# Routed experts on one core: where tiles of x1 wait, which queue loads unit 7 of W2, and when a piece of W1 is loaded

## What is computed

```python
grouped = x.reshape(b, s // g, g, d)                        # groups of g = 32 tokens
logits = jnp.einsum('bntd,des->bntes', grouped, Wc) + bc + tie
perm = (logits == jnp.max(logits, axis=-3, keepdims=True))  # each expert takes one token of each group
permuted = jnp.einsum('bntd,bntes->bnesd', grouped, perm)
inner = jax.nn.relu(jnp.einsum('bnesd,esdf->bnesf', permuted, W1) + b1)
result_permuted = jnp.einsum('bnesf,esdf->bnesd', inner, W2) + b2
result = jnp.einsum('bnesd,bntes->bntd', result_permuted, perm)
x = x + jnp.tanh(g_ffn[0]) * result                         # the input of this layer is layernorm(x)
```

## Time and profile before

| | us |
|---|---|
| median of 3 runs | 1896.14 |
| lowest and highest | 1892.81, 1897.17 |
| profiled execution, time | 1897.31 |
| profiled execution, span | 1895.3 |
| TensorE busy in the span | 1670.7 (88%) |
| VectorE busy | 1321.8 (70%) |
| ScalarE, POOL busy | 708.7, 752.8 |
| TensorE's mean granted clock | 0.944 |

### The profile page before, as it was taken

How to read it: one execution, slowest core, us unless ns; L and a number is a source line. 1 busy time by engine, 2 the same in 40 slices (tenths; PEclk the granted TensorE clock), 3 DMA queues, 4 the chain that set the end, 5 groups by cost and what they waited for, 6 DMA issues and landing times.

```text
span 1895.3 us, 51938 instructions
## 1 busy us (share of the span) xinstructions
PE 1670.7 (88%) x22488; PEld 1157.6 (61%) x22488; DVE 1321.8 (70%) x1944; ACT 708.7 (37%) x907; POOL 752.8 (40%) x896
## 2 busy tenths in 40 slices
PE   7899999999999999997797778887887888877985
PEld 4677777777777777775565435653465446543652
DVE  6677777777777777775376657676676567665766
ACT  3523333223332333322444344344434444434442
POOL 3467777777777777773111111111111111111101
PEclk9999999999999999998998899888998889888997
DMA  7533444444434444435665677566866686567655
GB/s 269 167 110 134 165 145 166 144 165 149 171 132 151 142 160 144 153 120 178 189 227 182 211 252 248 194 201 231 263 194 199 227 273 204 194 219 263 233 159 190
DMA packets 184435, 356.27 MB, mean 188 GB/s; under 512 B 23824, under 2 KB 33808, under 8 KB 178704
## 3 DMA queue, kind: packets, MB, share of 16 engines
q1 hardware_dynamic: 179600, 319.39, 50.9%
q10 hardware_dynamic: 4608, 33.56, 4.9%
HBM read 274.17 MB, written 78.71 MB: 186 GB/s over the span
## 4 chain that ended last, share of the span: by engine, by line
PE 58%; DMA 16%; DVE 11%; SPq 8%; issue 4%; ACT 2%; POOL 0%; DVEq 0%; ACTq 0%
PE ps L1400 14%; PE ps L877 10%; PE ps L924 10%; PE ps L1374 8%; DMA xin<-x_scratch 6%; DMA gat<-in_W 5%; PE ps L937 5%; DMA out<-gat 4%; SPq L1194 4%; PE ps L892 3%; PE ps L950 2%; DVE mx L675 2%; SPq L1190 2%; PE ps L1423 2%; PE ps L911 1%
## 5 line engine op out<-in xcount | busy, mean ns | idle before, releaser
L189 POOL TENSOR_SCALAR xin<-xin,r_all,nb_all 128x512 f32<-128x512 f32 x128 | 98.8, 781 | 624.2 <-DMA xin<-x_scratch 624.0
L1307 DVE STREAM_TRANSPOSE res<-res 128x2048 f32<-128x2048 f32 x128 | 292.0, 2295 | 0.1
L1278 ACT ACTIVATE res<-ps 128x1024 f32<-128x1024 f32 x160 | 157.9, 1024 | 288.8 <-PE ps L1423 288.8
L1268 ACT ACTIVATE gat<-ps 128x1536 f32<-128x1536 f32 (+1 forms) x128 | 172.2, 1345 | 214.2 <-PE ps L1374 214.2
L877 PE MATMUL ps<-xTh,qh 128*128 128x512 f32 x512 | 209.2, 409 | 5.5 <-DVE qs L692 1.9
L877 PE MATMUL ps<-xTh,ql 128*128 128x512 f32 x512 | 200.3, 391 | 0.0
L877 PE MATMUL ps<-xTl,qh 128*128 128x512 f32 x512 | 200.1, 391 | 0.0
L1374 PE MATMUL ps<-sel,xin 32*128 32x128 f32 x4096 | 158.9, 291 | 36.7 <-ACT gat L1268 22.5
L1418 PE MATMUL ps<-b2s,rowk 32*128 32x512 f32 x512 | 75.3, 573 | 128.8 <-DMA gat<-in_W 75.8
L1418 PEld LDWEIGHTS ps<-b2s,rowk 32*128 32x128 f32 x512 | 29.0, 208 | 254.5 <-DMA gat<-in_W 90.3
L1329 DVE COPY res<-ps 128x1024 f32<-128x1024 f32 x96 | 117.2, 1221 | 87.3 <-PE ps L1423 87.2
(11 more groups left out here) (152 smaller groups left out, 3319.1 us busy)
## 6 DMA issues: line engine op xcount, KB each, us to landing
xin<-x_scratch SPq DMA_DIRECT2D x196, 256.0 KB, 4.5
xT<-in_xT SPq DMA_DIRECT2D x32, 1024.0 KB, 6.0
xin<-in_x SPq DMA_DIRECT2D x64, 512.0 KB, 3.8
x_scratch<-xin SPq DMA_DIRECT2D x64, 512.0 KB, 3.0
xin<-in_W SPq DMA_DIRECT2D x128, 256.0 KB, 3.7
gat<-in_W ACTq DMA_DIRECT2D x32, 1024.0 KB, 6.8
xT<-in_W SPq DMA_DIRECT2D x68, 256.0 KB, 4.2
gat<-in_W SPq DMA_DIRECT2D x64, 256.0 KB, 5.0
```

The source lines that it names most:

```text
L189: e.tensor_scalar(self.xn[:, t, :], self.xn[:, t, :], self.r[:, i, t:t + 1], self.nb[:, i, t:t + 1], ALU.mult, ALU.add).then_inc(self.m_xn ...
L1268: e.activation(o, v, ACT.Copy).then_inc(m_gaA.sem, 1)
L1278: e.activation(o, v, ACT.Copy).then_inc(m_evA.sem, 1)
L1307: e.transpose(v, v).then_inc(m_tr.sem, 1)
```

## The change

x1 tiles 0 to 3 of batch i - 1 no longer go to `y` but to `xn`'s tiles 4 to 7, where the x of batch i was gathered from; so they wait for the last gather, tiles 2 and 3 also for 0 and 1 to land, and the x tiles 4 to 7 of batch i + 1 wait until they are stored. x1 tiles 4 to 7 go to `y`. `spare(i + 1)` holds unit 7 of W2 only, which ScalarE loads, 1 MB at once, after the last product of the first layer; unit 5 is loaded behind the first four relus, unit 6 behind the others. The middle piece of W1 waits for unit 7 of the batch before (unit 5 before). Unit copies go half to ScalarE and half to VectorE for all eight. The picks, POOL's second product and the bias products of the first layer stand at other places.

```diff
         d_room = {u: mark(f"room{u}", 1, 16) for u in W2_MOVED}
-        tile_of = lambda b, t: y[:, t] if t < NY else spare(b)[:, (t - NY) * D:(t - NY + 1) * D] if b < B - 1 else xn[:, t]
-        tiles_of_last = lambda h: xn[:, NY:2 * NY] if h else y
+        tile_of = lambda b, t: xn[:, NY + t] if t < NY else y[:, t - NY]
+        tiles_of_last = lambda h: y if h else xn[:, NY:2 * NY]
...
         def load_second(e, i, u):
-            e.wait_ge(m_w1.sem, m_w1.at(i, 5))
+            e.wait_ge(m_w1.sem, m_w1.at(i, 7 if u == W2_MOVED[2] else 5))
             e.dma_start(second(i, u), w2_dram[u].rearrange("p (k d) -> p k d", d=D)).then_inc(d_room[u].sem, 16)
...
             def load_middle(i, c):
                 if i:
-                    e.wait_ge(d_ys[c].sem, d_ys[c].at(i - 2))
-                    e.wait_ge(m_w2.sem, m_w2.at(i - 1, 5))
+                    e.wait_ge(d_ys[NY + c].sem, d_ys[NY + c].at(i - 2))
+                    e.wait_ge(m_w2.sem, m_w2.at(i - 1, 7))
...
             def load_x(i, t):
                 e.wait_ge(m_gap.sem, m_gap.at(i - 1, 2 * (C - 1) + t // TH))
+                if t >= NY and i >= 2:
+                    e.wait_ge(d_ys[t - NY].sem, d_ys[t - NY].at(i - 2))
...
             def load_y(b, t):
-                if t < NY and live(b + 1):
+                if t < NY:
+                    e.wait_ge(m_gap.sem, m_gap.at(min(b + 1, B - 1), 2 * C - 1))
+                elif live(b + 1):
                     e.wait_ge(m_w1.sem, m_w1.at(b + 1, piece(b + 1, W1_MIDDLE)))
-                    if b:
-                        e.wait_ge(d_ys[t].sem, d_ys[t].at(b - 1))
-                elif t < NY:
+                if b:
                     e.wait_ge(d_ys[t].sem, d_ys[t].at(b - 1))
-                elif live(b + 1):
-                    e.wait_ge(m_w1.sem, m_w1.at(b + 1, 7))
-                else:
-                    e.wait_ge(m_gap.sem, m_gap.at(b, 2 * C - 1))
+                if t % NY >= 2:
+                    e.wait_ge(d_yl[t - 2].sem, d_yl[t - 2].at(b))
...
-            def load_third(i, c):
-                ...
-                e.dma_start(quarter(spare(i + 1), c), quarter(w2_dram[W2_MOVED[2]], c)).then_inc(d_room[W2_MOVED[2]].sem, 16)
...
-                for what, t in (("x", 0), ("x", 1), ("y", 0), ("y", 1), ("x", 2), ("x", 3), ("y", 2), ("y", 3)):
+                for what, t in (("x", 0), ("x", 1), ("y", 4), ("y", 5), ("y", 0), ("y", 1), ("y", 2), ("y", 3), ("x", 2), ("x", 3), ("y", 6), ("y", 7)):
...
                 if live(i - 1) and i < B:
+                    for t in range(NY):
+                        store_y(i - 1, t)
+                if live(i + 1):
                     for t in range(NY, NT):
-                        load_y(i - 1, t)
-                if live(i + 1):
-                    for t in range(TH, NT):
                         load_x(i + 1, t)
                 if live(i - 1) and i < B:
-                    for t in range(NT):
+                    for t in range(NY, NT):
                         store_y(i - 1, t)
                 if live(i + 1):
                     route.load_logits(e, i + 1, 1)
-                if live(i):
-                    for c in range(QUARTERS):
-                        load_third(i, c)
...
                 route.scaled(e, i, 0)
-                for t in range(TH, NT):
+                route.normed(e, i, TH)
+                route.normed(e, i, TH + 1)
+                route.scaled(e, i, 1)
+                for t in range(TH + 2, NT):
                     route.normed(e, i, t)
-                route.scaled(e, i, 1)
...
                         for j in range(4):
                             hidden(i, j, p)
-                load_second(e, i, W2_MOVED[0])
-                for u, jp in W2_BY_ACT:
-                    rest(i, u, jp)
-                    if (u, jp) == (0, 0):
-                        load_second(e, i, W2_MOVED[1])
+                        load_second(e, i, W2_MOVED[p % 2])
+                    load_second(e, i, W2_MOVED[2])
+                for u in range(8):
+                    rest(i, u)
...
                     if live(i - 1) and i < B:
                         finish(i - 1, t)
-                for u, jp in W2_BY_DVE if live(i) else ():
-                    if live(i + 1) and (u, jp) == W2_BY_DVE[1]:
+                    if live(i + 1) and t == 4:
                         pick(i + 1, 0)
-                    if live(i + 1) and (u, jp) == W2_BY_DVE[4]:
+                for u in range(8):
+                    if live(i):
+                        rest(i, u)
+                    if live(i + 1) and u == 4:
                         pick(i + 1, 1)
-                    rest(i, u, jp)
...
-                        if n == 1:
+                        if n == 0:
                             bias(i)
```

More of the change, by code:

```diff
@@ L1070, in experts @@
         d_mid = [mark(f"mid{c}", 1, 16) for c in range(QUARTERS)]
-        d_room = {u: mark(f"room{u}", 1 if u < W2_MOVED[2] else QUARTERS, 16) for u in W2_MOVED}
+        d_room = {u: mark(f"room{u}", 1, 16) for u in W2_MOVED}
         m_gap, m_w1, m_w2, m_sc = mark("gap", 2 * C), mark("w1", 2 * C), mark("w2", 8), mark("sc", NT)
-        m_gaA, m_hr, m_evA = mark("gaA", 2 * C), mark("hr", 8), mark("evA", len(W2_BY_ACT))
-        m_gaV, m_evV, m_tr, m_fin = mark("gaV", 2 * C), mark("evV", len(W2_BY_DVE)), mark("tr", 8), mark("fin", NT)
+        m_gaA, m_hr, m_evA = mark("gaA", 2 * C), mark("hr", 8), mark("evA", 8)
+        m_gaV, m_evV, m_tr, m_fin = mark("gaV", 2 * C), mark("evV", 8), mark("tr", 8), mark("fin", NT)
         d_last = mark("last", 4, 16)
@@ L1139, in copied @@
         def copied(e, i, u):
-            e.wait_ge(m_evA.sem, m_evA.at(i, max(k for k, v in enumerate(W2_BY_ACT) if v[0] == u)))
-            for k, v in enumerate(W2_BY_DVE):
-                if v[0] == u:
-                    e.wait_ge(m_evV.sem, m_evV.at(i, k))
+            e.wait_ge(m_evA.sem, m_evA.at(i, u))
+            e.wait_ge(m_evV.sem, m_evV.at(i, u))
         def load_second(e, i, u):
-            e.wait_ge(m_w1.sem, m_w1.at(i, 5))
+            e.wait_ge(m_w1.sem, m_w1.at(i, 7 if u == W2_MOVED[2] else 5))
             e.dma_start(second(i, u), w2_dram[u].rearrange("p (k d) -> p k d", d=D)).then_inc(d_room[u].sem, 16)
@@ L1229, in sync @@
                     route.load_logits(e, i + 1, 1)
-                if live(i):
-                    for c in range(QUARTERS):
-                        load_third(i, c)
-            for t in range(NY, NT):
-                load_y(B - 1, t)
             three, rest_of = slice(0, 3 * P), slice(3 * P, D)
@@ L1303, in swap @@
                 if k == 0:
-                    e.wait_ge(m_evA.sem, m_evA.at(i, len(W2_BY_ACT) - 1))
-                    e.wait_ge(m_evV.sem, m_evV.at(i, len(W2_BY_DVE) - 1))
+                    copied(e, i, 7)
                 v = res[:, k // 2 * Q * P:(k // 2 + 1) * Q * P].rearrange("p (d2 m d1 j) -> p d1 d2 m j", m=Q // 2, d1=2, j=2)[:, k % 2]
@@ L1324, in pick, with rest @@
                 route.pick(e, i, h)
[L1326 removed]
+            def rest(i, u):
                 e.wait_ge(m_w2.sem, m_w2.at(i, u))
[L1328 removed]
+                o, v = pair_of(u, 1)
                 e.tensor_copy(o, v).then_inc(m_evV.sem, 1)
```

12 lines of the change are left out of this document (2 added, 10 removed).

## The result

The changed kernel takes 1970.9 us (median; 1969.7 to 1974.3), the kernel before 1896.7 beside it on the same chip: ratio 1.0394, 95% interval 1.0368 to 1.0420. It is 74 us slower. The forecast was 1954, with 1892 to 1992 as its range.

The account below looks back on a forecast made before the run. TensorE was taken as the engine to fill, idle 74.1 us on W2 unit 7's load; late second picks would cost more than that stall. 1897.3 + 14 x 4.3 (+60) - 3 at the edges = 1954 us, range 1892 to 1992.

Parts of the forecast that it names:

- The stall goes: TensorE before second-layer unit 7: its wait for the W2 load disappears, 5.58 us in the batch told.
- x1 2 and 3 block SyncE, the factors are issued at about 1411, 1 us after scatter's start: SyncE's queue: x1 waits hold it until 1407.5, so the first half's factors lose 3 us.
- Three loads in front, product 1 at +15.4: DMA queues: 3 MB of W2 ahead of small tiles; POOL's first product and first store's landing come at 1425.5.
- Chain from the first store to the second pick, 13.5 us: SyncE, then POOL: store, x loads, stores, second logits, product; the pick comes at 1439.0, against 1435.20 before.
- Pick to gather, 7.6: VectorE and TensorE: pick, next copy, unit 7 and transposes take 7.1 to 8.1 us; gather 4.3 us later.
- The path of the first pick is the upper bound: VectorE and TensorE: late first pick, last x1 tile at 1431.2, then six units; gather up to 6.8 us late.
- At nothing: First layer: late middle piece of W1, moved bias products, POOL's normalizing and ScalarE's copies cost no time.
- The sum: Whole kernel: 14 batches x 4.3 = +60 us, first and last batch together -3, giving 1954 us.
- A: Rival: queues absorb the loads, tile delay stays 7.8 us, gather 1.4 us earlier; 1875 us, chance 0.15.
- B: Rival: queues share by bytes, first store at 1422.7, gather 1.5 us later; 1915 us, chance 0.18.
- C: Rival: the two waits cancel, gather within 0.2 us of now; 1897 us, chance 0.05.
- D: Rival: first pick sets the end, half clock in second layer, +92 us; 1989 us, counted within the forecast's 0.62.

Follow-up runs that it names:

- w2_left_out: Changed kernel with units 5 to 7 of W2 loaded in the first batch only, 3 MB a batch left out: 1875.3 us, ratio 0.9905.
- u67_late: Changed kernel with ScalarE issuing unit 6 of W2 behind its copy of unit 0 and unit 7 behind its copy of unit 2: 1976.8 us, ratio 1.0436.
- pick2_last: Changed kernel with VectorE's second pick behind its copy of unit 7 instead of unit 4: 1984.9 us, ratio 1.0500.
- old_copies: Changed kernel with the division of copies and the second pick's place taken back to the kernel before, all loads as changed: 1960.2 us, ratio 1.0342.
- rebuilt_picks: Changed kernel with copies, picks and bias products placed as before, x1 2 and 3 unpaced, second logits earlier, units 6 and 7 later: 1847.5 us, ratio 0.9765.
- the three edits: Changed kernel, old copies, unit 6 late; edits: x1 2 and 3 unpaced, second logits before x 6, unit 7 behind ScalarE's unit 1 copy: 1857.6 us, ratio 0.9802.

## Why the prediction was right

By its own steps:

- *The stall goes*: right, and all of it.
- *x1 2 and 3 block SyncE, the factors are issued at about 1411, 1 us after scatter's start*: 1.4 on the mean. Right.
- *Three loads in front, product 1 at +15.4*: 14.3. The number was right; w2_left_out shows that the 3 MB make 7.4 us of it. My reason that they go in front packet for packet explains little of it: with packets of 1.8 KB the tiles beside the loads gained 2.0 to 2.8 us, but product 1 only 1.0. For the rule of the Trainium skill that I leaned on ("DMA: Bandwidth & Descriptors", section "Queues, rings and completion order") the runs are no clear evidence either way. That page counts a packet in descriptors; that their bytes don't matter was my reading of it, and no run here shows its packets. What the profile shows is that 256 KB beside one of these loads take about 8 us (7.8 in u67_late and in the earlier trace rows), and 12 to 13 with all three ahead (12.8 for the factors).
- *Chain from the first store to the second pick, 13.5 us*: the chain itself was right, 28.3 - 14.9 = 13.4 to the end of POOL's product. But it isn't what the pick waited for. In all 14 batches the pick started when VectorE had copied unit 4, at 29.7, 1.4 us after the product was done. This step took the wrong path for the limit.
- *Pick to gather, 7.6*: 37.0 - 29.7 = 7.3. Right.
- *The path of the first pick is the upper bound*: it is the path that sets the end, and in a way that the forecast hadn't followed. It took this path to run through units 1 to 6 straight to unit 7, up to 6.8 us late. Those units alone would have let unit 7 start at 31.6 (unit 6 starts at 30.0, and pick2_last has unit 7 at 31.7). But the path also passes through the copy of unit 4, the second pick and the copy of unit 5, and so unit 7 starts at 33.3. With the second pick at its product's end the gather would have come at about 28.3 + 7.3 = 35.6, 3.0 later than before instead of 4.4 (my estimate).
- *At nothing*: the middle piece of W1 was indeed never waited for. But the first layer grew by 0.9 us a batch, 12 us in all, of which 0.7 is idle time of TensorE. Most of that lies in pauses within the products of W1 that the profile calls "issue" (1.15 us a batch instead of 0.55). The loads of W2 aren't their cause (1.14 in w2_left_out), nor is the division of the copies (1.12 in old_copies), nor the place of the bias products (1.23 in rebuilt_picks, with these back). What the cause is stays open.
- *The sum*: 14 x 4.3 = 60 against 14 x 5.2 = 73: 4.4 from the gather, 0.9 from the first layer. The edges were not -3 but +1: the first scatter starts 5.1 us later than before (980.6 for 975.5) and the last part is 4.2 us shorter.
- *Rivals*: A (first store before 1421.2, that is +11.2) is out, it landed at 14.9. B would have had it at 12.7; it too is out. C is out by the 74 us. D had the right path (the first pick sets the end) and overpriced it: 6.8 us a batch against 4.4. The half clock that it named is there: scatter and second layer have 13.5 us at half clock a batch, 10.5 before.

The root of the loss was right: late loads ahead of the small tiles delay both products. Which of the two chains then holds the end was wrong, and that the number came near is in part luck: both chains start from the same late stretch and end 1.4 us apart, and the gather, taken 4.3 us later, came 4.4 later. The forecast was 17 us short of 74: 12 in the first layer taken at nothing, 4 in the edges, 1 in the gather.

## What to carry over

Before you remove a wait, look for what is due right behind it, and price the change by that: here the 5 us stall covered a pick that came 2.4 us before its end, and leaving the stall out bought nothing. When two chains reach the same end, look at the instruction in question for idle time before it: the second pick had none, and that says which chain it hung on. When an early load is put behind the work that frees its place, count whose small loads it will stand in front of, and who waits for those. And look hard at waits that only pace a queue: one of them was among the three edits that turned +2.6% into -2.0%. No run takes it out alone, so its share isn't shown.

## What the runs showed of the hardware

- A wait that moved later in TensorE's order took the slow clock with it. Without unit 7's load the gather started 1.8 us earlier, but 6.7 us of each first layer ran at 1.2 GHz, 1.0 us before; the first layer's busy time went from 26.6 to 28.6 us, and the batch took 62.0 us (61.9 before).
- A 256 KB load pays for the large loads around it. The first factors took 12.8 us from issue to landing with 3 MB of W2 in the queues (changed kernel), 7.1 with 1 MB (u67_late), 5.7 with none (w2_left_out); the first store 12.4, 6.5 and 5.1.
- Four loads of 256 KB instead of one of 1 MB, issued by ScalarE, landed later as a whole (unit 7 at 18.7 us after scatter's start instead of 12.0). The small tiles beside the first of them landed 2.0 to 2.8 us earlier, the factors and the first store behind them 1.0 and 0.4.
